# The 3x3 depthwise over sampled columns: from TensorE's product weights to nine VectorE taps a chunk

## What is computed

```python
for g in range(G):
    xi = x[..., g * Cg:(g + 1) * Cg]
    offsets = _conv_same(xi, off_w[g], off_b[g])
    ...
    sampled = _bilinear_sample(xi, loc)
    Kin = K * K * Cg
    s = sampled.reshape(B, H, W, Kin)
    s = _conv_same(s, dw_w[g], dw_b[g], groups=Kin)
    s = _conv_same(s, pw_w[g], pw_b[g])
    outs.append(s)
return jnp.concatenate(outs, axis=-1)
```

## Time and profile before

| | us |
|---|---|
| timed runs: median of 3 | 12,372.77 |
| timed runs: lowest, highest | 12,350.68, 12,377.28 |
| profiled execution: span | 17,350.5 |
| POOL busy, all of it | 8,759.5 |
| PE busy | 8,037.3 |
| DVE busy | 5,165.4 |
| ACT busy | 1,769.5 |
| granted TensorE clock, mean over the span, of full speed | 0.694 |

### The profile page before, as it was taken

How to read it: one execution, slowest core, us unless ns; L and a number is a source line. 1 busy time by engine, 2 the same in 40 slices (tenths; PEclk the granted TensorE clock), 3 DMA queues, 4 the chain that set the end, 5 groups by cost and what they waited for, 6 DMA issues and landing times.

```text
span 17350.5 us, 102336 instructions
## 1 busy us (share of the span) xinstructions
PE 8037.3 (46%) x30934; PEld 5581.5 (32%) x30934; DVE 5165.4 (30%) x5993; ACT 1769.5 (10%) x2822; POOL 8759.5 (50%) x9300
## 2 busy tenths in 40 slices
PE   4444444445345544443335555344325555443358
PEld 2223223223234432232224443232223443222245
DVE  2222222322333233233222233223223223222323
ACT  1001101110000011100000001110000001110014
POOL 4555555455554555455554455555555444545530
PEclk7667677667667776666667777666667777666679
DMA  2222222222223321222123321222112332122233
GB/s 78 68 60 66 78 62 70 72 61 77 61 75 98 98 60 48 63 80 59 43 61 99 98 84 45 57 77 68 46 52 77 98 98 61 48 64 77 60 124 118
DMA packets 878203, 1254.74 MB, mean 72 GB/s; under 512 B 183384, under 2 KB 663064, under 8 KB 859992
## 3 DMA queue, kind: packets, MB, share of 16 engines
q0 software_dynamic: 294912, 604.57, 13.7%
q1 hardware_dynamic: 511784, 596.71, 10.7%
q10 hardware_dynamic: 71344, 51.39, 0.9%
HBM read 1069.42 MB, written 245.43 MB: 76 GB/s over the span
## 4 chain that ended last, share of the span: by engine, by line
another core or an unknown queue 40%; PE 20%; issue 19%; DVE 10%; ACT 3%; PEldq 2%; PEld 1%; SPq 1%; DMA 1%; ACTq 1%; DVEq 1%
PE acc L1307 8%; PE stage L1163 6%; DVE srow L1685 5%; PE stage L1035 2%; PEldq L483 2%; DVE gathered L1678 2%; PE pt L1294 1%; ACT stt L1008 1%; PEld acc L1307 1%; PE stage L1102 1%; PE stage L1081 1%; DMA off<-offs 1%; DVE wtn L1647 0%; SPq L694 0%
## 5 line engine op out<-in xcount | busy, mean ns | idle before, releaser
L543 POOL DMA_INDIRECT gathered<-table,idx x9216 | 8708.9, 945 | 7844.0 <-issue 4412.7
L1307 PE MATMUL acc<-stt,room 128*128 128x256 f32 (+2 forms) x15360 | 4368.5, 438 | 4763.0 <-ACT stt L1008 2491.7
L1307 PEld LDWEIGHTS acc<-stt,room 128*128 128x128 f32 (+1 forms) x15360 | 3242.4, 221 | 5803.8 <-issue 2728.6
L1685 DVE TENSOR_REDUCE srow<-gathered 128x576 f32<-128x2304 f32 x512 | 2097.1, 4096 | 324.7 <-remote 207.2
L1163 PE MATMUL stage<-room 128*128 128x128 f32 x6784 | 1035.3, 303 | 1067.5 <-issue 1049.5
L1163 PEld LDWEIGHTS stage<-room 128*128 128x128 f32 x6784 | 962.5, 218 | 1139.8 <-issue 1134.0
L1678 DVE TENSOR_TENSOR gathered<-gathered,wtb 128x2304 f32<-128x2304 f32 x512 | 1304.4, 2548 | 1.2 <-issue 1.2
L1008 ACT ACTIVATE stt<-pt 128x1024 f32<-128x1024 f32 (+1 forms) x512 | 415.6, 812 | 8375.5 <-remote 4988.2
L1666 DVE SCALAR_TENSOR_TENSOR xs<-acc,fused,xr 128x256 f32<-128x256 f32 x128 | 61.7, 482 | 3747.9 <-PE acc L1307 2206.0
L1035 PE MATMUL stage<-room,mat 128*128 128x512 f32 (+1 forms) x1360 | 776.2, 694 | 841.1 <-issue 338.9
L1294 PE MATMUL pt<-mat,srow 128*128 128x128 f32 x2048 | 427.2, 337 | 1475.6 <-DVE srow L1685 1250.7
(11 more groups left out here) (212 smaller groups left out, 4575.2 us busy)
## 6 DMA issues: line engine op xcount, KB each, us to landing
gathered<-table,idx POOLq DMA_INDIRECT x9216
room<-toep SPq DMA_DIRECT2D x48, 1792.0 KB, 7.0
room<-toep SPq DMA_DIRECT2D x64, 1280.0 KB, 8.0
room<-toep SPq DMA_DIRECT2D x64, 768.0 KB
table<-room SPq DMA_DIRECT2D x64, 512.0 KB
toep<-in_taps SPq DMA_DIRECT2D x128, 224.0 KB
gathered<-toep SPq DMA_DIRECT2D x16, 1792.0 KB, 7.0
toep<-in_taps SPq DMA_DIRECT2D x128, 160.0 KB
```

The source lines that it names most:

```text
L543: nc.gpsimd.indirect_dma_start(gat[r][:, k % K9 * G + k // K9, :], None, table[b].rearrange("(n e) -> n e", e=PAIR), bass.IndirectOffsetOn ...
L1307: ins = nc.tensor.matmul(sums_of[:, pairs, :], wk[0:kk, m, dx, at:at + P], stt[0:kk, slots, m, dx:dx + W], start=start and m == 0 and dx == 0,
L1685: nc.vector.tensor_reduce(srow[r % 2][:].rearrange("p (s c) -> p s c", c=CG), gat[r][:].rearrange("p s (q c) -> p s c q", q=4), AX.X, ALU. ...
```

## The change

The depthwise convolution leaves PE's weights. ACT copies the turned columns into a ring of rows (`ring`, eleven rows a chunk; first and last rows of a step twice, so that each step finds its neighbours). One step later DVE computes the depthwise itself (`depthwise_taps`): for each of the five chunks nine taps over four rows of 128 pixels, the first a multiplication by a scalar for each partition, the other eight a multiplication and an addition to a running sum `taps_of`, all in SBUF; each waits for the one before. The ninth writes `dwo`, one of two buffers. PE then does only the pointwise product (`pointwise`), two matmuls a chunk. Chunks 0 and 1 stand behind row 1 of the next step, 2 and 3 behind row 2, chunk 4 behind row 3 (`CHUNKS_AT`). A step's sums are therefore finished two steps later, not one, and SP's stores and loads move with them. In the last step all five chunks follow the last row. POOL no longer makes `wk`. The core of the diff:

```diff
+NROW = 2 * ROWS + 2
+COPIES = 6
+COPIED = (2, 3, 4, 6)
+CHUNKS_AT = {1: (0, 1), 2: (2, 3), 3: (4,)}
...
-                for m in range(MCH):
-                    for dy in range(3):
-                        for dx in range(3):
-                            nc.gpsimd.tensor_scalar(wk[:, m, dx, (3 - dy) * C:(4 - dy) * C], pw[:, m, 0:C],
-                                                    dw[:, m, 3 * dy + dx:3 * dy + dx + 1], None, ALU.mult)\
-                                .then_inc(wk_ready, 1)
...
-                            if not (isinstance(n, int) and n == 0):
-                                store_pairs(n - 1)
-                            load_pairs(n)
+                            if not (isinstance(n, int) and n < 2):
+                                store_pairs(n - 2)
+                            if not (isinstance(n, int) and n < 1):
+                                load_pairs(n - 1)
...
                     for r in range(ROWS):
-                        yield 3 * r + 2
                         v = n * ROWS + r
+                        yield 3 * r + 2 if r < ROWS - 1 else 11.6
+                        act.wait_ge(tap_done, MCH * (n + 1 if r < ROWS - 1 else n + 2))
                         act.wait_ge(turned_full, v + 1)
-                        act.wait_ge(rows_used, v + 1)
-                        nc.scalar.activation(stt[:, SLOT_OF[r], 0:4, 1:W + 1], over_slots(r, pt[:]), ACT.Copy)\
-                            .then_inc(full_ready, 1)
+                        copy_full(4 * (i % 2) + r + 1, pt[:])
+                        if r in (0, ROWS - 1):
+                            row, edge = again(r, i)
+                            copy_full(row, none_full if edge else pt[:])
...
-                        for dx in range(3):
-                            ins = nc.tensor.matmul(sums_of[:, pairs, :], wk[0:kk, m, dx, at:at + P],
-                                                   stt[0:kk, slots, m, dx:dx + W], start=start and m == 0 and dx == 0,
-                                                   stop=True, skip_group_check=True)
-                    return ins
+                def pointwise(n, m):
+
+                    if m == 0:
+                        pe.wait_ge(pair_added, n + 1)
+                    pe.wait_ge(tap_done, MCH * (n + 2) + m + 1)
+                    for par in range(2):
+                        ins = nc.tensor.matmul(sums_of[par * C:(par + 1) * C, :, :], pw[:, m, 0:C],
+                                               dwo[m % 2][:, par:ROWS:2, :], start=(m == 0), stop=(m == MCH - 1))
+                    ins.then_inc(pw_done, 1)
...
+                def depthwise_taps(n, half, m):
+
+                    kk = P if m < MCH - 1 else C
+                    if m == 0:
+                        copied = COPIES * (n + 1) + (COPIED[0] if not (isinstance(n, int) and n == STEPS - 1) else 1)
+                        dve.wait_ge(full_ready, copied)
+                        dve.wait_ge(rest_ready, copied)
+                    for t in range(K9):
+                        rows = ring[0:kk, m, ds((4 * half + t // 3) * PADW, ROWS * PADW)]
+                        src = rows.rearrange("p (r w) -> p r w", w=PADW)[:, :, t % 3:t % 3 + W]
+                        w = dw[0:kk, m, t:t + 1]
+                        if t == 0:
+                            ins = ts(taps_of[0:kk], src, w, None, ALU.mult)
+                        elif t < K9 - 1:
+                            ins = stt_(taps_of[0:kk], src, w, taps_of[0:kk], ALU.mult, ALU.add)
+                        else:
+                            dve.wait_ge(pw_done, MCH * n + m + 1 if m > 1 else MCH * n + 2 - m)
+                            stt_(dwo[m % 2][0:kk], src, w, taps_of[0:kk], ALU.mult, ALU.add).then_inc(tap_done, 1)
+                            dve.wait_ge(tap_done, MCH * (n + 2) + m + 1)
+                            break
+                        ins.then_inc(tapped, 1)
+                        dve.wait_ge(tapped, (K9 - 1) * (MCH * n + m) + t + 1)
...
-                        if r == 1 and not (isinstance(n, int) and n == 0):
-                            finish(n - 1)
+                        if r == 0 and not (isinstance(n, int) and n < 2):
+                            yield 2.5
+                            finish(n - 2)
+                        if r and not (isinstance(n, int) and n == 0):
+                            yield 3 * r + 2.4
+                            for m in CHUNKS_AT[r]:
+                                depthwise_taps(n - 1, (i + 1) % 2, m)
                     if last:
+                        yield STEP
+                        finish(n - 1)
+                        for m in range(MCH):
+                            depthwise_taps(n, i % 2, m)
                         finish(n)
```

More of the change, by code:

```diff
@@ L177, in drive @@
             span = STEP / stage.parts
+            if done == 1:
+                assert stage.steps == 1
+                weave(step(n + 1, b, 1),
+                      *(timed(part[f](at, stage.first + q), span * q, span / stage.phases)
+                        for q in range(stage.parts) for f in stage.flows if f in part))
+                leave(stage, at)
+                done += 1
+                continue
             with eng.Fori(0, stage.steps) as j:
@@ L276, in build @@
         room = sb("room", [P, ROOM + N_WK + N_KEPT])
-        wk = room[:, ROOM:ROOM + N_WK].rearrange("p (m x c) -> p m x c", m=MCH, x=3)
-        at = [ROOM + N_WK]
+        at = [ROOM]
         def carve(*shape):
@@ L286, in carve @@
             return a.rearrange(f"p ({names}) -> p {names}", **{f"d{i}": k for i, k in enumerate(shape[:-1])})
+        ring, dwo = carve(MCH, (NROW + 1) * PADW), [carve(ROWS, W) for _ in range(2)]
+        pw, dw, taps_of = carve(MCH, P), carve(MCH, K9), carve(ROWS, W)
         def several(n, *shape):
@@ L994, in close, with at_row, copy_full @@
                         act.dma_start(out[:, ds(n(u) * TILE, TILE)], res[u]).then_inc(res_out[u], 16)
-                def over_slots(r, a):
-                    at = SLOT_OF[r]
-                    return a.unsqueeze(1).to_broadcast([a.shape[0], len(range(at.start, at.stop, at.step or 1)), *a.shape[1:]])
+                def at_row(k):
+                    return ds(k * PADW + 1, W)
+                def copy_full(k, src):
+                    nc.scalar.activation(ring[:, 0:MCH - 1, at_row(k)], src, ACT.Copy).then_inc(full_ready, 1)
@@ L1001, in step, with copy_rest, again @@
+                def copy_rest(k, src):
+                    nc.scalar.activation(ring[0:C, MCH - 1, at_row(k)], src, ACT.Copy).then_inc(rest_ready, 1)
+                none_full, none_rest = zero[:].unsqueeze(1).to_broadcast([P, MCH - 1, W]), zero[0:C, :]
+                def again(r, i):
+                    half, edge = i % 2, isinstance(i, int) and i == (0 if r == 0 else PER - 1)
+                    return (NROW - 1 + half if r == 0 else NROW * (1 - half)), edge
                 def step(n, b, i):
@@ L1015, in _ @@
+                        if r in (0, ROWS - 1):
+                            row, edge = again(r, i)
+                            copy_rest(row, none_rest if edge else pr)
+                    if isinstance(n, int) and n == STEPS - 1:
+                        yield STEP
+                        copy_full(NROW - 1, none_full)
+                        copy_rest(NROW - 1, none_rest)
                 act.sem_inc(so_s, 2)
@@ L1314, in step @@
-                    full, rest = range(MCH - 1), (MCH - 1,)
                     for r in range(ROWS):
-                        v = n * ROWS + r
                         yield 3 * r + 2
[L1318 to L1335, removed]
-                                                     stop=True, skip_group_check=True)
-                            products(r, slots, pairs, full[:1], start=r == 1 and not first)
-                            turn_rest(r)
-                            yield 3 * r + 4
-                            products(r, slots, pairs, full[1:])
-                            pe.wait_ge(st_ready, v + 1)
-                            products(r, slots, pairs, rest).then_inc(rows_used, 1)
@@ L1727, in _ @@
                 dve.sem_inc(pair_added, 1)
+                dve.sem_inc(tap_done, 2 * MCH)
                 dve.sem_inc(res_s, 1)
```

72 lines of the change are left out of this document (38 added, 34 removed).

## The result

The changed kernel takes 13,218.4 us (median of four runs, 13,214.1 to 13,222.1) against 12,374.8 for the kernel before on the same chip: 1.0684 times as long, interval 1.0669 to 1.0699. It is slower by 844 us. The forecast was 13,285 us, range 12,900 to 13,600.

A forecast was written before the change was run, and what follows sets the result against it. POOL, issuing gathers almost without a pause, was taken to bound the timed runs. 12,373 us, plus 885 for gathers held by taps, plus 27 for the last step, gave 13,285 us; range 12,900 to 13,600.

The forecast's parts named there:

- The base: Timed runs: POOL issues gathers almost without a pause, 12,342 us against the 12,373 median; the profiled execution's stalls are its own.
- What it removes: PE's 15,360 product matmuls (4,368.5 us) and POOL's 45 weight products (19 us) go; both save nothing.
- What it adds: 45 taps a step on DVE, 34.1 us; 78 us of DVE in 90 fits and alone costs nothing.
- What the taps do to POOL: Taps with two SBUF inputs hold gathers in flight: 1.570 us each, 7.0 us a step, 885 us in all.
- the gap is 0.035 and a tap's period 0.785: DVE's chained taps: 0.75 us each plus the pause read from four chained operations; a held gather then costs 1.570 us.
- the second rival: Two SBUF inputs don't hold gathers, only a first tap does: 12,560 us, or 12,400 with no delay; chance 0.09.
- The order of work: First rival: PE waits for taps, ACT and DVE for PE, in depthwise steps; 312 us more, about 13,600; chance 0.18.
- the 14.7 us: First rival: 96 of 120 band matmuls at 0.153 us behind waits for taps, making DVE's step about 95 against POOL's 97.
- the single duration of 0.303: First rival: at this time per band matmul, 29 us instead of 14.7, a step of 110 and 312 us more.
- the sign that the forecast named for this rival: For the first rival: POOL stalled for DVE's reductions in a timed total beyond 13,480 us.
- The last step: The last step's taps have no cover: 44 us where 17 stood before, so 27 us more.

The follow-up runs named there:

- both costs mended: The changed kernel with the taps' running sum in idle PSUM and PE's pointwise products issued later, behind the turning of the row's last chunk: 12,376.8 us, ratio 1.0021.
- the run with unread taps: The kernel before, PE's products kept, plus 45 DVE taps a step whose result nobody reads, running sum in SBUF: 13,097.5 us, ratio 1.0602.

## Why the prediction was right, and where two errors met

*The base.* That POOL bounds the timed runs, and that the stalls of the profiled execution were its own, held: span 12,346.1 above, with all of PE's products in it, and no gaps.

*What it removes* was costed at nothing, rightly: some 3,000 us of PE less, and with both costs mended 26 us slower than before. (POOL's weight products take 18.6 us in the earlier trace rows, so 0.41 each, not 0.43.)

*What it adds.* A tap was put at 0.75 us, the first at 0.50: 0.76, 0.75 and 0.50 in the rows. DVE's busy time was put at some 9,300: 9,348.8.

*What the taps do to POOL.* The mechanism is shown by two pairs of runs that differ in the sum's memory: 751 us without the change, 530 with it (12,906.3 to 12,376.8). **The size was off:** the term gave 885 us, and about 550 was measured (581, less the 29 that the kernel has without SBUF taps). The step that failed is "the gap is 0.035 and a tap's period 0.785". That gap came from four operations of one stretch. In the change, 634 chunks of taps run beside gathers: 129 have this period throughout, and in 505 every pause is long, 0.14 us or, for about one in six, 0.23. The two kinds can be compared in one trace. Gathers that start within a chunk are held 1.17 us in sum at the short period, and 0.79 at the long one, though such a chunk lasts 7.85 us instead of 6.81.

Why a longer period costs less can in part be worked out. A gather that starts 0.16 to 0.45 us into a tap ends 0.818 us after that tap's end (1,492 such gathers beside L1711, deviation 0.003), and one that starts in a tap's first 0.09 us takes 0.946 (838 of them). After a held gather the next starts 0.818 + 0.305 = 1.123 after the tap's end. At a period of 0.785 that is 0.30 into a tap: held again, one gather in two periods, 1.570. At 0.897 it is 0.084 into a tap, and free; the one behind it starts 0.436 into the next and is held: two gathers in three periods, 1.345 each. Late by 0.096 instead of 0.321, that is 2.7 us a step of 38.2 us of taps. The cheapest steps of the change show 2.4 to 3.1, but five chunks at the long period cost 5 x 0.79 = 3.9 in the mean. Their periods are not all 0.897, most lie between 0.88 and 0.98; the remainder is not worked out. The mean of all steps is 4.6, against 7.0 in the forecast.

At the short period the term was too large as well, 7.0 a step against 5 x 1.17 = 5.9: the run with unread taps has 782 - 29 = 753, since a chunk of 6.8 us holds not 4.3 gathers of 1.25 to 1.30 us but 3.3 (2,081 in 635 chunks). By these means per chunk some 140 of the 335 us that the term had too much come from this, and some 195 from the long pauses.

This also mends the reading of the earlier trace rows, where a held gather was taken to end 0.09 us behind the second operation. It ends 0.82 behind the first; with operations 0.73 apart the two can't be told apart.

The Trainium skill ("SBUF — State Buffer", section "SBUF: two separate sides") lets an operation with two SBUF inputs lock GpSimd out only against one that reads SBUF. By the pairs of runs an indirect gather that POOL issues counts as one that is locked out, where its box names only operations in a two-port mode. The first taps fit the box as well, if they run in such a mode, which no row names: they have one SBUF input and take 0.50 us, and 35 gathers that started 0.16 to 0.30 us into one ended 0.816 after it, so the second rival's first taps hold gathers too, only not alone.

*The order of work.* The forecast took it for covered, "that buffers for four rows let DVE lag by some 60 us speaks against" it, and put it at 0.18 as the first rival with 24 steps at 110 us and 312 us. It came: 283 us, in steps of 110 to 117 us, 15 of the 24 in three images. The rival had the place right (PE waits for taps, band matmuls stand behind that wait, DVE waits for what they give). But the 14.7 us that left it just under POOL's step rest on a wrong count. A depthwise step has not 120 band matmuls but 240, and 192 of them stand behind the waits for taps, in two stretches:

```profile
4198.55 11.43 PE L1187 MATMUL stage<-room 128*128 128x128 f32 x80
...
4233.30 14.71 PE L1187 MATMUL stage<-room 128*128 128x128 f32 x112
```

That is 26 us, not 14.7. By the forecast's own 0.153 us each, 192 make 29 us: with DVE's 78 and ACT's part about 110, above POOL's 97, with no need for the single duration of 0.303. The 312 us came near the 283 by luck, too: half the matmuls at twice their time, and 24 steps of 13 us instead of 17 steps of 17. No engine is full in such a step; the line gives the window, its length and busy time and instructions of PE, its loads, DVE, ACT and POOL, then clock, DMA share and GB/s:

```profile
4167.94:4280.66 112.72, 45.17 (x286) 38.94 (x285) 76.12 (x95) 11.26 (x22) 72.37 (x72) 0.64 0.38 124
```

It is a ring of waits through programs of fixed order, and moving one wait on PE opened it. And the sign that the forecast named for this rival, a total beyond 13,480, would have missed it.

*The last step.* 27 us forecast, 30 in the column "end".

So 12,353 + about 550 + 283 + 30 = 13,216, against 13,218 measured. The forecast's 13,285 is near because 335 us too much in one term met 283 too little in another. What the forecast gave for the sign was sound; its closeness was luck.

## What to carry to other kernels

Where GpSimd issues the DMAs that set the pace, look at where VectorE's wide operations have their operands before counting their microseconds: the same 45 taps a step cost 750 us with the sum in SBUF and nothing with it in PSUM. When an engine of fixed order gets a new wait, list what stands behind it in its program, counted in the trace, and who waits for that; the cure can be to issue the waiting product a little later. And undo suspected costs together as well as singly: alone, the two overlapping costs here seemed worth 312 and 377 us, together they were worth 842.

## What the runs showed that I had not expected

- A chain of taps of 0.75 us with pauses of 0.14 us costs POOL less than one with 0.03, at the same work: in the changed kernel 0.79 against 1.17 us a chunk, and with a sixth of the unread taps slowed 13,050.3 against 13,097.5 us. The gathers fall into step with the taps, and a step of two gathers in three taps is better than one in two.
- A held gather takes the rest of the tap and then 0.818 us more, within 0.003 us; an operation of 0.31 us, as in the earlier trace rows, can therefore hardly delay one of 0.944 (by at most some 0.09 us, an estimate from these numbers).
- The first tap, one input and a scalar, takes 0.50 us from SBUF to SBUF and 0.74 from SBUF to PSUM, and in the second form it holds no gather (62 that started 0.16 to 0.30 us into one took 0.944). The sum's memory costs DVE 0.25 us a chunk here and saves POOL far more.
- The ninth tap in the run with the sum in PSUM reads one input from SBUF, one from PSUM, and writes SBUF; beside it too gathers take 0.944 us. So what matters in a two-input tap is where the inputs lie, not where the result goes.
